# The last three sublayers of an eight-sublayer transformer stack as one stream of 24 items

## The reference

```python
def rotary(x):                       # L1_attn_b, 16 heads of 16 features
    q, k, v = rope(x @ Wq + bq), rope(x @ Wk + bk), x @ Wv + bv
    p = softmax(causal(q @ k.T / 4))
    return (p @ v) @ Wo + bo
    # rope(z) = z * cos + [-z[8:], z[:8]] * sin, in each head of 16

def ffn(h):                          # L1_ffn, hidden width 1024
    a = attention(rmsnorm(h) * ln1)              # 16 heads of 16, causal, @ Wo
    mod = 0.1 * tanh(a @ A)
    h2 = rmsnorm(h) * ln2
    gate = silu(h2 @ W_in.T + mod * (h2 @ A) @ B)
    return h + (gate * (h2 @ W_up.T)) @ W_down.T

x = x + ffn(layernorm(x)); x = x + rotary(layernorm(x)); x = x + ffn(layernorm(x))
```

## Time and profile before

| | us |
|---|---|
| median of 3 runs (lowest, highest) | 3744.82 (3743.2, 3748.74) |
| profiled execution: first to last instruction | 3744.3 |
| first feed-forward call, first scores to last residual | 2593.4 to 2983.4 |
| rotary call, first scores to last residual | 3006.4 to 3325.1 |
| second feed-forward call, first scores to last residual | 3348.0 to 3736.5 |
| PE busy over the span | 91% |

### The profile page before, as it was taken

How to read it: one execution, slowest core, us unless ns; L and a number is a source line. 1 busy time by engine, 2 the same in 40 slices (tenths; PEclk the granted TensorE clock), 3 DMA queues, 4 the chain that set the end, 5 groups by cost and what they waited for, 6 DMA issues and landing times. The chain is left out here.

```text
span 3744.3 us, 88994 instructions
## 1 busy us (share of the span) xinstructions
PE 3417.2 (91%) x35122; PEld 2784.6 (74%) x35122; DVE 2364.8 (63%) x6005; ACT 1895.3 (51%) x4671; POOL 800.3 (21%) x814
## 2 busy tenths in 40 slices
PE   6989888999999999999997898997999877769998
PEld 5777766888888888888886677775788755547887
DVE  4666646787877787777774566665555455645554
ACT  3555435666666666666663454554444233434442
POOL 2332312222222232222232232321000010100000
PEclk9999989999999999999998899998999988979999
DMA  5000000000000000000001200000000000000000
GB/s 214 1 1 1 1 9 19 20 22 19 19 19 19 19 19 19 19 19 19 19 19 58 106 1 1 1 1 1 1 1 1 1 1 1 1 1 1 1 1 23
DMA packets 51616, 67.75 MB, mean 18 GB/s; under 512 B 4994, under 2 KB 40322, under 8 KB 49666
## 3 DMA queue, kind: packets, MB, share of 16 engines
q1 hardware_dynamic: 51202, 62.05, 5.2%
HBM read 59.48 MB, written 2.56 MB: 17 GB/s over the span
## 5 line engine op out<-in xcount | busy, mean ns | idle before, releaser
L1285 DVE SCALAR_TENSOR_TENSOR d_acc<-d_raw,d_taps,d_acc 128x255 f32<-128x255 f32 (+2 forms) x1152 | 642.8, 599 | 146.7 <-ACT d_raw L1275 133.1
L1510 ACT COPY d_power<-bank 128x768 f32<-128x768 f32 x320 | 259.0, 810 | 217.2 <-PE bank L1503 217.2
L2291 ACT ACTIVATE m_probs<-bank,m_nmax 128x128 f32<-128x128 f32 (+1 forms) x512 | 166.2, 436 | 266.0 <-DVE m_nmax L2283 266.0
L1273 ACT ACTIVATE d_acc<-bank,d_tap_bias,d_taps 128x256 f32<-128x256 f32 x384 | 196.0, 561 | 167.1 <-PE bank L1254 160.6
L698 POOL TENSOR_TENSOR a_q<-a_rope 64x512 f32<-64x512 f32 x128 | 163.3, 1276 | 277.0 <-DVE a_rope L688 236.6
L738 ACT ACTIVATE a_area<-bank,a_nmax 128x128 f32<-128x128 f32 x256 | 93.6, 366 | 174.6 <-DVE a_nmax L729 174.4
L688 DVE TENSOR_TENSOR a_rope<-bank,a_sinT 32x512 f32<-32x512 f32 x256 | 177.4, 693 | 5.7
L765 ACT COPY a_area<-bank 128x512 f32<-128x512 f32 (+1 forms) x260 | 138.3, 580 | 73.6 <-PE bank L756 72.5
L675 PE MATMUL bank<-a_latT,a_wq 128*128 128x256 f32 x512 | 166.9, 408 | 6.7 <-DVE a_rope L688 4.5
L183 POOL TENSOR_TENSOR rstd<-var_eps,minus_half 128x2 f32<-128x2 f32 x64 | 45.9, 717 | 554.9 <-DVE var_eps L165 418.6
L1313 POOL TENSOR_TENSOR d_qT<-d_acc,d_sigm 128x512 f32<-128x512 f32 x64 | 84.4, 1319 | 368.0 <-ACT d_sigm L1295 368.0
(11 more groups left out here) (294 smaller groups left out, 9370.7 us busy)
## 6 DMA issues: line engine op xcount, KB each, us to landing
d_alpha<-d_alpha_rows SPq DMA_DIRECT2D x64, 256.0 KB, 3.5
d_g_decay<-d_running_rows SPq DMA_DIRECT2D x32, 258.0 KB, 3.4
a_w_o<-in_a_w_o SPq DMA_DIRECT2D x2, 2048.0 KB, 16.6
a_area<-in_a_q_nope SPq DMA_DIRECT2D x2, 1536.0 KB, 8.1
x<-in_x SPq DMA_DIRECT2D x8, 256.0 KB, 16.6
d_wk<-in_d_wk SPq DMA_DIRECT2D x1, 2048.0 KB
d_wq<-in_d_wq SPq DMA_DIRECT2D x1, 2048.0 KB
d_wv<-in_d_wv SPq DMA_DIRECT2D x1, 2048.0 KB
```

Source lines behind the costliest of these rows:

```text
L1273: nc.scalar.activation(acc[:, r % 3, j], b_proj[:, j * T:(j + 1) * T], ACT.Identity, scale=taps[:, r // 2, h, 3:4], bias=tap_bias[:, r // ...
L1285: last = nc.vector.scalar_tensor_tensor(out=acc[:, r % 3, j, d:T], in0=raw[:, r % 2, j, 0:T - d], scalar=taps[:, r // 2, h, 3 - d:4 - d], ...
L1510: nc.scalar.copy(power[:], b_step[:, :, 0:3 * P]).then_inc(g.step_out, 1)
L2291: last = nc.scalar.activation(probs[:, s % 2, i, cols], heads[:, i, cols], ACT.Exp, bias=nmax[:, s % 2, t, i:i + 1])
```

## The change

`small_sublayer` is replaced by `small_stream`, which goes through the 24 items (8 first feed-forward, 8 rotary, 8 second feed-forward) in one order written out as `ORDER`: five feed-forward items of the first sublayer, then rotary items with feed-forward items between them, then four of the last sublayer. No barrier stands between them. Each of the 24 items still has four slots. `closing_jobs` puts the hidden steps of a feed-forward item into the four slots right behind its own, and the output product of a rotary item into the one right behind it. A side step may belong to an item of another kind.

Other parts: the exchange of halves is done by DVE (`stream_shuffle` over partitions) on the projected and biased queries and keys instead of by a second projection. ACT adds the bias, POOL multiplies by the cosine and adds, DVE multiplies by the sine. Two slots share one transposed output tile (16 instead of 32 rows for a head), so that the output product and the modulation have two chunks of weights instead of four. All side steps, both kinds, use bank 7. The order of the side steps is now: second round of queries and keys of the item itself, tokens, first round, v of the next item. Each batch is stored when its last item is done.

```diff
+FFN, ROTARY = "F", "R"
+ORDER = ([(FFN, b) for b in range(5)] +
+         [(ROTARY, 0), (FFN, 5), (ROTARY, 1), (FFN, 6), (ROTARY, 2), (FFN, 0), (ROTARY, 3), (FFN, 7),
+          (FFN, 1), (ROTARY, 4), (FFN, 2), (ROTARY, 5), (FFN, 3), (ROTARY, 6), (ROTARY, 7)] +
+         [(FFN, b) for b in range(4, NB)])
+ITEMS = len(ORDER)
+SLOTS = ITEMS * SETS
+RANK = [sum(kind == ORDER[j][0] for kind, _ in ORDER[:j]) for j in range(ITEMS)]
+F_ITEMS = [j for j in range(ITEMS) if ORDER[j][0] == FFN]
+TOKENS_DEEP = 8
+MOD_DEEP = 4
+OT_DEEP = 3
+def closing_jobs():
+    jobs, free = {}, 0
+    for j, (kind, _) in enumerate(ORDER):
+        for n in range(HIDDEN_STEPS if kind == FFN else 1):
+            free = max(free, SETS * (j + 1))
+            jobs[free] = (kind, j, n)
+            free += 1
+    return jobs
+JOBS = closing_jobs()
+ALL_SLOTS = max(JOBS) + 3
...
-        w.q_swap, w.k_swap = (w.load(n, [P, KC, ROUNDS, P]) for n in ("wqs", "wks"))
-        w.bias_qk = w.load("bias_qk", [P, 4, ROUNDS])
+        w.bias_qk = w.load("bias_qk", [P, 2, ROUNDS])
...
-        w.o = w.load("wo", [P, SETS, D])
...
+        def bias_act(act, j, r_):
+            m = ROUNDS * RANK[j] + r_
+            need(act, g.qk_in_psum, ROUNDS * j + r_ + 1)
+            need(act, g.shuffled, m)
+            need(act, g.cos_ready, m)
             for n in range(2):
-                nc.vector.scalar_tensor_tensor(
-                    out=rope1[:, n], in0=b_gate[:, n * T:(n + 1) * T], scalar=bias_qk[:, n, r_:r_ + 1],
-                    in1=cos[:, n], op0=ALU.add, op1=ALU.mult)
-                last = nc.vector.scalar_tensor_tensor(
-                    out=rope2[:, n], in0=b_up[:, n * T:(n + 1) * T],
-                    scalar=bias_qk[:, 2 + n, r_:r_ + 1], in1=sin[:, n], op0=ALU.add, op1=ALU.mult)
-            last.then_inc(g.qk_products.sem, 1)
-        def rope_pool(pool, b, r_):
-            after(pool, g.qk_products, ROUNDS * b + r_ + 1)
-            after(pool, g.scores_in_psum, SETS * (b - 1))
-            after(pool, g.qk_ready, ROUNDS * (b - 1))
-            nc.gpsimd.tensor_tensor(qk[:, b % 2, r_], rope1[:], rope2[:], ALU.add)\
-                .then_inc(g.qk_sum.sem, 1)
+                last = nc.scalar.activation(biased[:, n], b_side[:, n * T:(n + 1) * T], ACT.Identity,
+                                            bias=wr.bias_qk[:, n, r_:r_ + 1])
+            last.then_inc(g.biased, 1)
+        def rotate_dve(dve, j, r_):
+            m = ROUNDS * RANK[j] + r_
+            need(dve, g.biased, m + 1)
+            need(dve, g.qk_sum, m)
+            nc.vector.stream_shuffle(flat(sines[:]), flat(biased[:]), [i ^ (HD // 2) for i in range(32)])\
+                .then_inc(g.shuffled, 1)
+            need(dve, g.shuffled, m + 1)
+            nc.vector.tensor_tensor(sines[:], sines[:], wr.sin[:], ALU.mult).then_inc(g.sin_ready, 1)
+        def rotate_pool(pool, j, r_):
+            m = ROUNDS * RANK[j] + r_
+            need(pool, g.biased, m + 1)
+            need(pool, g.qk_sum, m)
+            nc.gpsimd.tensor_tensor(cosines[:], biased[:], wr.cos[:], ALU.mult)\
+                .then_inc(g.cos_ready, 1)
+            need(pool, g.cos_ready, m + 1)
+            need(pool, g.sin_ready, m + 1)
+            need(pool, g.scores_in_psum, SETS * (j - 1))
+            need(pool, g.qk_ready, ROUNDS * (j - 1))
+            nc.gpsimd.tensor_tensor(qk[:, j % 2, r_], cosines[:], sines[:], ALU.add)\
+                .then_inc(g.qk_sum, 1)
+        def rotary_query_act(act, j, r_):
+            need(act, g.qk_sum, ROUNDS * RANK[j] + r_ + 1)
+            own_rows_act(act, j, r_, qk[:, j % 2, r_, 0]).then_inc(g.qk_ready, 1)
...
+        def side_free(pe, j, k):
+            if k == 0:
+                if is_ffn(j):
+                    need(pe, g.qk_ready, ROUNDS * j + 2)
+                elif is_rotary(j):
+                    need(pe, g.biased, ROUNDS * RANK[j] + 2)
+                elif is_ffn(j - 1):
+                    need(pe, g.modh_ready, RANK[j - 1] + 1)
+            elif j + 1 < ITEMS:
+                if k == 1:
+                    pe.wait_ge(*core.xnT_ready(j, 1))
+                elif k == 2 and is_ffn(j + 1):
+                    need(pe, g.qk_ready, ROUNDS * (j + 1) + 1)
+                elif k == 2:
+                    need(pe, g.biased, ROUNDS * RANK[j + 1] + 1)
+                else:
+                    need(pe, g.v_ready, j + 2)
+        def side_pe(pe, j, k):
+            s = SETS * j + k
+            if k == 0 and 0 <= j < ITEMS:
+                if is_ffn(j - 1):
+                    need(pe, g.modh_ready, RANK[j - 1] + 1)
+                elif s > 0:
+                    need(pe, g.turned, s)
+                else:
+                    need(pe, g.v_ready, 1)
+                qk_pe(pe, j, 1)
+            elif k > 0 and -1 <= j < ITEMS - 1:
+                if s > 0:
+                    need(pe, g.turned, s)
+                elif k > 1:
+                    side_free(pe, j, k - 1)
+                if k == 1:
+                    xnT_pe(pe, j + 1)
+                elif k == 2:
+                    qk_pe(pe, j + 1, 0)
+                else:
+                    v_pe(pe, j + 1)
...
+            need(dve, g.oT_ready, s // 2)
+            nc.vector.tensor_tensor(blocks(scaled[:])[:, :, cols], blocks(turned[:])[:, :, 0:HD],
+                                    recip[:].broadcast_to([P, T // VW, HD]), ALU.mult)\
+                .then_inc(g.scaled, 1)
+            if k % 2 == 1:
+                need(dve, g.scaled, s + 1)
+                if is_ffn(j - OT_DEEP):
+                    need(dve, g.mod_in_psum, RANK[j - OT_DEEP] + 1)
+                elif is_rotary(j - OT_DEEP):
+                    need(dve, g.y_steps, last_y(j - OT_DEEP))
+                nc.vector.transpose(oT[:, j % OT_DEEP, k // 2], scaled[:]).then_inc(g.oT_ready, 1)
...
+            for n, (w, act) in enumerate(((wf.oa, oT[:, j % OT_DEEP]), (wf.a2, xT[:, j % TOKENS_DEEP]))):
+                for c in range(KC):
+                    last = nc.tensor.matmul(b_side[:, n * T:(n + 1) * T], w[:, c], act[:, c],
+                                            start=(c == 0), stop=(c == KC - 1))
...
+        FIRST = -SETS - 1
...
+                for s in range(FIRST, ALL_SLOTS):
+                    j, k = s // SETS, s % SETS
+                    mod = k == 0 and s <= SLOTS and is_ffn(j - 1)
+                    if 0 <= s < SLOTS:
                         scores_pe(pe, s)
                     if 0 < s <= SLOTS:
                         pv_pe(pe, s - 1)
+                    if hidden_at(s):
+                        gate_up_pe(pe, *hidden_at(s))
                     if mod:
+                        need(pe, g.turned, s)
+                        mod_pe(pe, j - 1)
+                    elif s < SLOTS:
+                        side_pe(pe, j, k)
+                    if 0 <= s < SLOTS:
                         transposes_pe(pe, s)
+                    if mod and s < SLOTS:
+                        side_pe(pe, j, k)
+                    if hidden_at(s):
+                        modulate_pe(pe, *hidden_at(s))
+                    if hidden_at(s - 1):
+                        down_pe(pe, *hidden_at(s - 1))
+                    if out_at(s - 1) is not None:
+                        out_pe(pe, out_at(s - 1))
...
+            @block.sync
+            def _(sp):
+                for j in range(ITEMS):
+                    b = ORDER[j][1]
+                    if not any(ORDER[i][1] == b for i in range(j + 1, ITEMS)):
+                        need(sp, g.residual_done, j + 1)
+                        sp.dma_start(out[b], core.x[:, b]).then_inc(g.stored, 16)
+                sp.wait_ge(g.stored, 16 * NB)
...
-            small_sublayer(core, small, True, 0, w_ffn)
-            small_sublayer(core, small, False, 1, w_rope)
-            small_sublayer(core, small, True, 2, w_ffn)
-        done = ctx.enter_context(nc.semaphore("stored"))
-        with nc.Block() as block:
-            @block.sync
-            def _(sp):
-                for b in range(NB):
-                    sp.dma_start(out[b], core.x[:, b]).then_inc(done, 16)
-                sp.wait_ge(done, 16 * NB)
...
+            small_stream(core, w_ffn, w_rope, out)
```

837 lines of the change are left out of this document (357 added, 480 removed).

## The result

The changed kernel takes 3620.93 us (median of 4 runs, 3617.56 to 3622.36), the kernel before 3744.01 us (4 runs, 3738.48 to 3748.74): a ratio of 0.9669, 95% interval 0.9656 to 0.9683, or 123 us less. The forecast was 3603 us with a range of 3588 to 3655. The mechanism came out as told; the time is 18 us above the forecast, and one step of the prediction accounts for most of that.

A forecast was written before the change was run, and what follows sets the result against it. PE's matmuls bound steady feed-forward slots, the chain through the engines the rotary call. From 2574.3 us, 16.1 + 33.5 + 675.0 + 266.2 + 33.3 + 3.8 = 1027.9 us instead of 1170.0, giving 3603 us, range 3588 to 3655.

The forecast's parts named there:

- start: Ahead of the first scores: one round of queries and keys instead of two, 16.1 us instead of 19.10.
- first item: The first item's four slots: 33.5 us instead of 35.4, v leaving the second slot and a round entering the first.
- 15 dense items: Items beside hidden steps: PE-bound sets of 45.92 us, less eight trailing down products of 1.73 us, sum 675.0 us.
- 8 thin items: Items of the chain alone, without hidden steps: 32.65 us a set, plus 5 us of clock dips, 266.2 us.
- lie under PE: Items beside hidden steps: the rotation's new steps are free, PE having 10 to 13 us of work in a slot.
- failed cover: If PE's work did not hide the rotation's steps beside hidden steps: 16 rotations by at most 1.8 us = 29 us.
- the rotary sets' share: Part of the gain from faster rotary sets: 318.7 - 266.2 = 52 us.
- Rival 1: Stretches without hidden steps keep the rotary pace, 39.8 us a set: 52 us more, 3655; chance 0.13.
- Rival 2: Bank 7 becomes a serial resource: 0.5 us in each of 60 slots, 30 more, 3633; chance 0.14.
- Rival 3: Half-speed clock carried into hidden steps, dense sets 91.8 us; four such sets give 3787, slower than before; chance 0.035.
- Rival 4: No measurable change: 142 us of new waits, 1.5 us in each of the 96 slots; chance 0.015.
- The excluded pair: DVE's two-SBUF-input sine product waits for POOL's cosine product; in six rotations without hidden steps, 6 us, outside the sum.

The follow-up runs named there:

- the last pair: Changed kernel with r ahead, later rotation in dense rotary items and earlier products in thin items: mixed order 3586.51 us, sublayers' order 3610.38 us.

## Why the prediction was right in its mechanism and 18 us short

| term | forecast | measured |
|---|---|---|
| start | 16.1 | 15.6 |
| first item | 33.5 | 34.1 |
| 15 dense items | 675.0 | 693.3 |
| 8 thin items | 266.2 | 265.0 |
| last hidden steps | 33.3 | 33.4 |
| store | 3.8 | 2.4 |
| all, from 2574.3 us | 1027.9 | 1043.8 |

The terms are 15.9 us above the forecast; the other 2 us are that this median lies 2.8 us above the profiled span, where I had added 0.5 and rounded up.

**The step that failed** is the sentence that the rotation's new steps "lie under PE" and "are free while PE has 10 to 13 us of work in a slot". It is the term of the dense items: 21.4 us for the seven rotary ones. (Three feed-forward ones that follow a thin item, 1, 13 and 21, add 0.75 us with second slots of 10.33. The rotation isn't the reason, for item 1 has none near it: PE waits 0.18 us for the same hidden values there, behind the masking and copying that ACT does ahead of its gate.) I had argued from busy shares: DVE has time to spare in a slot. It has, but not at the moment that counts. PE's work in a slot is cut in two by the hidden values, and ahead of the cut it has the scores and the value product alone, 2.3 us (plus a trailing down product of 1.73 us in items 5 and 14, which for that reason lose 1.10 instead of 4.49). What is queued on DVE ahead of that cut is covered by these 2.3 us, not by 10 to 13. Ask of each waiting instruction what PE still has to do before it, not what the slot holds. The cause is shown from both sides: r taken out of the queue gives 11.34 us, the rotation taken out gives 10.19, and r shortened in its place gives 11.87.

I had priced a failed cover at 16 rotations by at most 1.8 us = 29 us. Only seven rotations met a hidden step, but four of them cost 2.5 times that price, as the matmuls behind a wait of 2.73 us ran at a lower clock: in that slot the full-clock matmuls need 10.1 us, the wait is 2.7, and the remaining 1.8 us are half-speed matmuls.

**A counting error with the other sign.** The last item has no item behind it that would need its side steps. Its slots are 13.1, 9.64, 9.65 and 9.65 us, 42.04 together, where I took 45.92: 3.9 us less. Without it the excess would have been seen whole: 21.4 + 0.75 - 3.9 = 18.3, the difference of the dense terms.

**Right.** Four of the dense feed-forward items, to the hundredth; in the three named above only the second slot is off, by 0.25 us, and the last item is shorter by the counting error. The thin items: 32.47 us undisturbed (32.65 forecast), and four dips of 1.3 to 1.6 us, 5.7 together, where I had taken 5; that it was four is luck, for the versions above have from none to six. The first item, 34.1 us against 33.5, is met by luck as well: its third slot dips to a clock of 0.61 and takes 10.66 us, and the same item takes 30.83 us where r stands ahead. Start and end. That the exchange costs 0.73 us, inside the bounds of 0.45 and 1.82 and near my 0.89. By cause, the rotary sets' share was put at 52 us, and the kernel before with only its two lists changed gains 52 in the medians and 48.5 in the rotary call. The two are not made of the same parts, though: that run still has the second projection.

**The rivals.** Rival 1 (rotary pace in thin stretches) is false: 32.5 to 33.9 us a set, not 39.8. Rival 2 (bank 7) is false in dense items, where PE never waits for that bank; in thin ones PE's 1.5 us ahead of the side step is a wait for the turned output, and other products fit into it. Rival 3 is false: no dense feed-forward item runs under the full clock, and where a dense rotary item does, its own wait came first. Rival 4 is false.

**The excluded pair.** In the changed kernel r takes 1.62 us with POOL's addition beside it, and 0.60 with that held back and all else in place; the sine product takes 1.09 beside POOL's cosine product and 0.69 without. The sine product has two SBUF inputs, and for it the trace agrees with what the Trainium skill states ("SBUF — State Buffer", on the shared port pair). The r products have one such input each, so the rule for two inputs, as I had taken it up, doesn't name them; for them the run that holds POOL back is the evidence. I had read the page, weighed it only for the sine product in thin items, priced it at 6 us and left it out of the sum. It acted in dense items, and most of all on an instruction that the change doesn't touch. By the run that holds POOL back the meeting with r cost 12.9 us in the dense slots, and 17 us in the medians with the dips that went along.

**Open.** Why a thin slot with the same instructions dips in one version and not in another (8.22 or 9.78 us). It follows neither the length of PE's wait in that slot, 1.5 us in both, nor its work alone; edits in the slots before it decide, and no run here isolates which. The value of the mixed order hangs on it: 14 us slower than the sublayers' order in the changed kernel, 5 us faster once r is ahead (in the sublayers' order its place matters to one dense rotary item only, and that has no excess), 24 us faster in the last pair, where one run of four in the sublayers' order came within 5.3 us. (In the profiled runs of that pair, 5 us of the difference lie ahead of the stream.)

## What to carry to other kernels

Busy shares don't say whether new work on a side engine is covered: find PE's first instruction in the slot that waits for that engine, and compare the queue ahead of what it waits for with PE's work ahead of it. Keep an in-order engine's list such that what the bounding engine waits for comes first, and look at which GpSimd instruction will run beside each VectorE one; a short product that isn't part of the change can become the long one. And before restructuring calls into a stream, try the same work in another order in its list: here that gave 52 us without the change, beside its 123, and 18 more behind it.

## What the runs showed of the hardware that I had not expected

- VectorE beside GpSimd: two TENSOR_SCALAR of 128x256 f32, 0.60 us, took 1.62 us while GpSimd added 128x512 f32 (1.26 us); a TENSOR_TENSOR of 128x512 went from 0.69 to 1.09 us, and one of 128x128 from 0.29 to 0.93 us. GpSimd's own instruction took 1.26 to 1.28 us in all of these.
- STREAM_SHUFFLE of 128x512 f32 took 0.73 us, with a LOAD_MASK_SELECT of 14 ns ahead of it.
- After a stop of 2.73 us in a busy stretch PE's next matmuls ran at a mean clock of 0.61 over 4.4 us, most of them at the lower level; after one of 1.72 us in the same place the slot stayed at 1.00. But thin slots with two waits, of 1.5 and 0.6 us, ran at 1.00 in one version and at 0.83 in another.
- A store of 256 KB closed the kernel in 2.4 us, against 7.8 us for eight at once.
